# Row factors of the attention output through DRAM instead of through TensorE, and four buffers with another number of homes

## The reference

```python
q = (x @ Wq).reshape(B, T, H, 2 * DH)        # B 4, T 1024, H 16, DH 32
k = (x @ Wk).reshape(B, T, KV, 2 * DH)       # KV 4, each used by 4 query heads
v = (x @ Wv).reshape(B, T, KV, 2 * DH)
q1, q2, k1, k2 = halves of q and k, each rotated (RoPE)
a1 = softmax(q1 @ k1.T * scale + causal mask)
a2 = softmax(q2 @ k2.T * scale + causal mask)
out = (a1 - lam * a2) @ v
out = group norm over (T, 2 * DH) per head, * gn_w + gn_b
x = layernorm(x + (out * (1 - LAMBDA_INIT)) @ Wo)
up, gate = x @ ternary(W_up).T, x @ ternary(W_gate).T
x = layernorm(x + (silu(up) * gate) @ ternary(W_down).T)
```

## Time and profile before

| | |
|---|---|
| time, median of 3 runs | 2199.38 us (2192.79 to 2201.3) |
| the profiled execution, its own time | 2201.01 us |
| its span in the trace | 2196.6 us |
| TensorE busy | 2125.6 us, 97% |
| VectorE busy | 1688.4 us, 77% |
| ScalarE busy | 1458.0 us, 66% |
| GpSimd busy | 1194.4 us, 54% |
| mean granted clock of TensorE | 0.992 |

### The profile page before, as it was taken

How to read it: one execution, slowest core, us unless ns; L and a number is a source line. 1 busy time by engine, 2 the same in 40 slices (tenths; PEclk the granted TensorE clock), 3 DMA queues, 4 the chain that set the end, 5 groups by cost and what they waited for, 6 DMA issues and landing times.

```text
span 2196.6 us, 41181 instructions
## 1 busy us (share of the span) xinstructions
PE 2125.6 (97%) x13314; PEld 1367.8 (62%) x13314; DVE 1688.4 (77%) x3701; ACT 1458.0 (66%) x3450; POOL 1194.4 (54%) x1919
## 2 busy tenths in 40 slices
PE   8999999999999999999999999999999999999998
PEld 4666666666665766666666666666666666654443
DVE  4888888889888887788887888878778788853333
ACT  0777777667776777777667777777677687742232
POOL 0577666677655655555654655655455555531232
PEclk9999999999999999999999999999999999999999
DMA  7666576757655512212462322342552212114000
GB/s 252 200 210 219 195 216 198 238 180 221 189 163 149 163 51 61 92 50 62 145 153 79 97 68 84 96 125 73 154 116 54 73 40 87 49 49 110 6 20 19
DMA packets 291217, 263.85 MB, mean 120 GB/s; under 512 B 65088, under 2 KB 233152, under 8 KB 288960
## 3 DMA queue, kind: packets, MB, share of 16 engines
q1 hardware_dynamic: 279808, 228.65, 35.6%
q10 hardware_dynamic: 11200, 32.58, 4.6%
HBM read 181.48 MB, written 71.30 MB: 115 GB/s over the span
## 4 chain that ended last, share of the span: by engine, by line
PE 77%; DVE 8%; POOL 5%; issue 5%; ACT 4%; DMA 1%; ACTq 0%; DVEq 0%; SPq 0%; POOLq 0%
PE PS L1171 18%; PE PS L1120 11%; PE PS L1101 10%; PE PS L1082 10%; PE PS L1140 9%; PE PS L1161 9%; PE PS L1180 8%; PE PS L1147 2%; DVE e_long L1458 2%; POOL linv L1383 2%; ACT dt_long L1222 1%; ACT e_long L1232 1%; POOL coef L1384 1%; PE PS L1086 1%; DVE e_long L1524 1%
## 5 line engine op out<-in xcount | busy, mean ns | idle before, releaser
L1383 POOL TENSOR_TENSOR linv<-lsum,powers 128x2 f32<-128x2 f32 x512 | 405.7, 792 | 415.5 <-ACT e_long L1232 340.2
L1232 ACT ACTIVATE e_long<-e_long,nmax 128x768 f32<-128x768 f32 (+3 forms) x512 | 505.2, 987 | 159.5 <-DVE nmax L1458 156.8
L1458 DVE CUSTOM_DVE_ANT_0 e_long<-PS,mask_b 128x768 f32<-128x768 f32 (+3 forms) x512 | 516.8, 1019 | 82.1 <-PE PS L1101 61.0
L1101 PE MATMUL PS<-kstk,qstk 128*128 128x384 f32 (+5 forms) x1536 | 479.0, 416 | 19.6 <-DVE nmax L1458 9.5
L1101 PEld LDWEIGHTS PS<-kstk,qstk 128*128 128x128 f32 x1536 | 269.7, 191 | 144.5 <-issue 83.8
L1222 ACT ACTIVATE dt_long<-PS 128x512 f32<-128x512 f32 (+3 forms) x544 | 258.4, 514 | 136.5 <-PE PS L1082 126.5
L1524 DVE SCALAR_TENSOR_TENSOR e_long<-e_long,coef 128x1024 f32<-128x1024 f32 (+3 forms) x256 | 276.6, 1080 | 68.4 <-POOL coef L1384 68.0
L1232 ACT ACTIVATE e_short<-e_short,nmax 128x384 f32<-128x384 f32 (+3 forms) x512 | 283.1, 557 | 20.1 <-DVE nmax L1458 19.4
L1396 POOL TENSOR_TENSOR hid<-th,hid 128x512 f16<-128x512 f32 x128 | 148.2, 1160 | 248.8 <-ACT hid L1272 129.6
L1384 POOL TENSOR_SCALAR coef<-lsum,linv,neglam 128x1 f32<-128x1 f32 x512 | 233.2, 456 | 53.4
L1082 PE MATMUL PS<-ident,e_long 128*128 128x128 f32 x1664 | 239.6, 276 | 13.9 <-DVE nmax L1458 7.1
(11 more groups left out here) (117 smaller groups left out, 3114.9 us busy)
## 6 DMA issues: line engine op xcount, KB each, us to landing
qstk<-dq SPq DMA_DIRECT2D x512, 128.0 KB, 2.9
dq<-hl SPq DMA_DIRECT2D x25, 1024.0 KB, 5.1
wr<-in_w_proj ACTq DMA_DIRECT2D x48, 512.0 KB, 5.1
kstk<-dk SPq DMA_DIRECT2D x64, 256.0 KB, 5.2
da<-ra SPq DMA_DIRECT2D x32, 512.0 KB, 3.3
at_sb<-da SPq DMA_DIRECT2D x32, 512.0 KB, 4.3
wt<-in_w_up SPq DMA_DIRECT2D x16, 512.0 KB, 6.0
wt<-in_w_gate SPq DMA_DIRECT2D x16, 512.0 KB, 5.5
```

The source lines that it names most:

```text
L1101: last = nc.tensor.matmul(slot[:, h, :], qstk[:, duo % 4, 2 * r + m, :].bitcast(F32R), kstk[:, g % 2, m, h * w:(h + 1) * w].bitcast(F32R), ...
L1232: nc.scalar.activation(e, e, ACT.Exp, bias=nmax[:, u % 8:u % 8 + 1], scale=-1.0, accum_out=lsum[:, n % 4, m:m + 1]).then_inc(s_exp, 1)
L1383: link(nc.gpsimd.tensor_tensor(linv[:, a % 8, :], lsum[:, a % 4, :], mone, ALU.pow))
L1458: nc.vector.tensor_tensor_reduce(out, slot, mask, -1.0, -NEG, ALU.add, ALU.min, nmax[:, u % 8:u % 8 + 1]).then_inc(s_negmax, 1)
```

## The change

The columns of `linv` are no longer spread and transposed. SP stores the two columns of a duo to a row pair in DRAM (`store inverses`: 128 x 2 elements of 4 bytes), waits until they have landed, and loads each row of 128 factors into 64 partitions of `inverses` (`load inverses`: two DMAs, four homes). The product on VectorE reads them there, after a wait for the landing (`s_rows`). The POOL copy, the transposition, the extra block of the eviction and `r_short` are gone, and with them the waits of evictions for products. `e2_long` gets a second home, so that the minimum of a long head's second map waits for the combine two long heads back and no longer for that of the previous long head. `coef` gets four columns for two, `qstk` three homes for four, and `xT` four for six. The planner's durations and conditions follow, so that all five lists are made anew.

```diff
@@
-X_HOMES = 6
+X_HOMES = 4
@@
-    home = (4 * h + c + 4) % X_HOMES
-    return home, B - 1 if home < 4 else h
+    return c, B - 1 + h
@@
-            if STEPS[back].r:
-                out.append(ITEM("product", STEPS[back].duo))
-        if STEPS[a].r and not in_line(STEPS[a].duo) and STEPS[a].duo >= 8:
-            out.append(ITEM("product", STEPS[a].duo - 8))
@@
-            out.append(ITEM("combine", a - 2))
+            out.append(ITEM("combine", a - 2 if a % 2 or a < 4 else a - 4))
@@
-        out = [ITEM("values", run_of(a))]
+        out = [ITEM("values", run_of(a)), ITEM("load inverses", a)]
@@
+    elif what == "store inverses":
+        out = [ITEM("factor", heads_of(a)[1])] + [ITEM("load inverses", a - 4)] * (a >= 4)
+    elif what == "load inverses":
+        out = [ITEM("store inverses", a)] + [ITEM("product", a - 4)] * (a >= 4)
@@
-        if a >= 4:
-            out.append(ITEM("scores", heads_of(a - 4)[1], 1))
+        if a >= 3:
+            out.append(ITEM("scores", heads_of(a - 3)[1], 1))
@@
+            def store_inverses(duo):
+                second = heads_of(duo)[1]
+                sp.wait_ge(s_coef, second + 1)
+                sp.dma_start(dinv[duo].rearrange("r q -> q r"), linv[:, (second - 2) % 8:second % 8 + 1:2, 0],
+                             allow_slow_non_contiguous=True)\
+                    .then_inc(s_inv[duo % 4], 16)
+
+            def load_inverses(duo):
+                inverses_stored(sp, duo)
+                if duo >= 4:
+                    multiplied(sp, duo - 4)
+                for r in range(2):
+                    sp.dma_start(inverses[64 * r:64 * r + 64, duo % 4, :], dinv[duo, r:r + 1, :].broadcast_to((64, P)))\
+                        .then_inc(s_rows[duo % 4], 16)
@@
-                if blocks > keys:
-                    duo = STEPS[n].duo
-                    pe.wait_ge(s_wide, duo + 1)
-                    last = nc.tensor.transpose(F[bank][:, keys * P:blocks * P],
-                                               wide[:, duo % 2, :, :].rearrange("p r d -> p (r d)"), ident[:, :])
                 last.then_inc(s_tb, 1)
@@
-                if here < blocks:
-                    copied = nc.scalar.activation(r_short[:, :], F[bank][:, here * P:blocks * P], ACT.Copy)
@@
-                        nc.gpsimd.tensor_copy(wide[:, duo % 2, :, :], linv[:, (a - 2) % 8:a % 8 + 1:2, 0:1]
-                                              .broadcast_to((P, 2, 64))).then_inc(s_wide, 1)
@@
-                if m == 1 and n >= 2:
+                if m == 1 and n % 2 and n >= 2:
                     dve.wait_ge(s_comb, n - 1)
+                elif m == 1 and n >= 4:
+                    dve.wait_ge(s_comb, n - 3)
@@
-                    rows = dt_of(heads_of(a)[1])[:, t + 1, :] if in_line(a) else r_short[:, :]
+                    dve.wait_ge(s_rows[a % 4], 32 * (a // 4 + 1))
                     dve.wait_ge(s_pv, run_of(a) + 1)
```

More of the change, by code:

```diff
@@ L392, in after @@
         out = [ITEM("exponent", a, 1), ITEM("minus lambda")]
-        if STEPS[a].r and STEPS[a].duo >= 2:
-            second = heads_of(STEPS[a].duo - 2)[1]
-            out.append(ITEM("turn", second, turns(second) - 1))
+        if a >= 8:
+            out.append(ITEM("store inverses", STEPS[a - 8].duo))
+    elif what == "store inverses":
+        out = [ITEM("factor", heads_of(a)[1])] + [ITEM("load inverses", a - 4)] * (a >= 4)
+    elif what == "load inverses":
+        out = [ITEM("store inverses", a)] + [ITEM("product", a - 4)] * (a >= 4)
     elif what == "hidden low":
@@ L478 @@
            [ITEM("store rotated", j) for j in O_JOBS], [ITEM("load q", duo) for duo in range(DUOS)],
+           [ITEM("store inverses", duo) for duo in range(DUOS)], [ITEM("load inverses", duo) for duo in range(DUOS)],
            [ITEM("turn x", j) for j in OF_KIND["wo"]], [ITEM("load k", g) for g in range(B * KV)], [ITEM("load v", g) for g in range(B * KV)],
@@ L489 @@
 AHEAD = {"minimum": 1.0, "exponent": 1.0, "evict": 1.5, "factor": 2.0, "combine": 0.6, "empty": 3.0, "copy": 2.0,
-         "sum": -1.5, "ternary": -1.5, "side": -1.0, "rsqrt": 1.0, "product": 0.5, "load q": 2.0, "store rotated": 3.0}
+         "sum": -1.5, "ternary": -1.5, "side": -1.0, "rsqrt": 1.0, "product": 0.5, "load q": 2.0, "store inverses": 1.5, "load inverses": 1.5, "store rotated": 3.0}
 NTH = 4
@@ L745, in layer_kernel @@
         linv = sb("linv", [P, 8, 2])
-        coef = sb("coef", [P, 2])
-        dt_long = [sb(f"dt_long{r}", [P, NT + r, P]) for r in range(2)]
+        coef = sb("coef", [P, 4])
+        dt_long = [sb(f"dt_long{r}", [P, NT, P]) for r in range(2)]
         dt_short = sb("dt_short", [P, 3, NT // 2, P])
-        r_short = sb("r_short", [P, P])
-        wide = sb("wide", [P, 2, 2, 64])
+        inverses = sb("inverses", [P, 4, P])
         ra = sb("ra", [P, 2, T])
@@ L847, in layer_kernel @@
         s_pv = sem("s_pv")
-        s_wide = sem("s_wide")
+        s_inv = [sem(f"s_inv{k}") for k in range(4)]
+        s_rows = [sem(f"s_rows{k}") for k in range(4)]
         s_short = sem("s_short")
@@ L1046, in _ @@
                     load_q(a)
+                elif what == "store inverses":
+                    store_inverses(a)
+                elif what == "load inverses":
+                    load_inverses(a)
                 elif what == "load k":
@@ L1100, in scores @@
                 for h in range(parts):
-                    last = nc.tensor.matmul(slot[:, h, :], qstk[:, duo % 4, 2 * r + m, :].bitcast(F32R),
+                    last = nc.tensor.matmul(slot[:, h, :], qstk[:, duo % 3, 2 * r + m, :].bitcast(F32R),
                                             kstk[:, g % 2, m, h * w:(h + 1) * w].bitcast(F32R), start=True, stop=True)
```

70 lines of the change are left out of this document (28 added, 42 removed).

## The result

The changed kernel takes 3162.9 us (median of 4 runs, 3145.8 to 3187.0) against 2197.5 us; the ratio is 1.440, 95% interval 1.429 to 1.452. I had forecast 2172 us.

What follows compares the result with a forecast made beforehand. TensorE, busy 2125.6 of 2196.6 us, was taken as the bound. Less 28.2 us, all other terms 0, the span is 2168.4; plus 4.4 outside, less 1.6 for the median, 2171, rounded to 2172 us; range 2148 to 2203.

Steps and rivals of the forecast that it cites:

- the price of the store: Store of factors to DRAM: 2.1 us from issue to landing, within a trip of 5.6 us.
- Rival D: Store's 256 small elements go one after another at 45 ns, trip 17 us, VectorE stands: over 2500 us; chance 0.05.
- the DMA engines' share: DMA engines: 98 304 new packets at 45 ns, 277 us on each of 16 engines; room enough.
- TensorE's part: TensorE's list: 256 transpositions go at 0.11 us each, nothing takes their place: -28.2 us.
- The trip: Factors through DRAM to VectorE's product: 5.6 us, hidden under an even duo's 8.8 us lag; term 0.
- rival C: Late products hold up VectorE's minima, 192 us idle at 0.14 us each: +27 us, 2199 us; chance 0.17.
- Homes, 0: Changed homes for q, x and long second maps: loads still arrive in time, TensorE waits for none; 0.
- Rival B: Second home and freed evictions take away half of 44 us TensorE idle time: 2150 us; chance 0.14.
- Rival E: Three q homes and SP's in-order waits make TensorE wait for q, 51 us: 2223 us; chance 0.07.
- The tail, F: Feed-forward work moves into the tail, 97 to 100% busy, and costs nothing; no chance of its own.

Runs made afterwards that it cites:

- e5: The change with its stores issued but loads not waiting for them and reading another input; only the factor 8 heads later waits: 2739.7 us (1.247).
- e11: Kernel before with all lists unchanged, 192 of 256 transpositions of the spread factors left out: 2184.2 us (0.9942).
- e2: Kernel before with all homes of the change and lists made for them, factors still going through TensorE: 2254.0 us (1.0256).
- e1: The change without the store to DRAM and the wait for it; loads stay but read another input: 2229.9 us (1.0145).
- e16: Kernel before, four x homes, other lists kept, 192 transpositions out, SP given waited stores 64 bytes apart and loads of another input: 2252.4 us (1.0248).
- e9: Kernel before with four homes for x instead of six and nothing else changed: 2196.9 us (0.9997).
- e15: Kernel before with four x homes, two for long second maps and four coef columns, planner not told, lists kept: 2195.6 us (0.9988).
- e8: Kernel before with three homes for q instead of four and nothing else changed, lists made for it: 2213.6 us (1.007).
- e21: As e16, but with the change's own store of neighbouring elements and loads of the true factors: 3122.1 us (1.422).
- e12: e2 with the planner's PACE 3.85 instead of 3.75 us a head: 2251.3 us (1.0242).
- e6: The change with the store's 4-byte elements 64 bytes apart in DRAM, waiting loads reading another input: 2258.9 us (1.028).
- e13: The change's trip without its new homes, store elements 64 bytes apart, waiting loads reading another input, new lists: 2240.4 us (1.0197).
- e10: Kernel before with four x homes, two for long second maps and four coef columns, planner told, new lists: 2247.4 us (1.0234).
- e14: Kernel before with the planner's PACE 3.85 instead of 3.75 us a head: 2221.1 us (1.011).
- e23: Kernel before with the planner's PACE 3.76 instead of 3.75, only lists differing: 2203.8 us (1.0041).

## Why the prediction was wrong

**The step that failed is the price of the store.** I took 2.1 us from `out<-x`, with 3.3 us as the upper end, "because the store has only 1 KB". The change's store lands 9.9 us behind its issue in the median, and the whole trip of an even duo takes 17.5 us for my 5.6. Rows of large stores can't bound one of neighbouring 4-byte elements from above; bytes were the wrong measure to find the nearest row by. With elements 64 bytes apart the landing takes 2.4 us: for such a store 2.1 would have been near. Rival D, at 0.05, had the outcome (over 2500 us, from a landing more than 3 us late) and the wrong mechanism: it priced packets one after another at 45 ns, and they took 9 ns in parallel. The rule that I weighed, the Trainium skill's in "DMA: Bandwidth & Descriptors", section "Specifications", that transfers under 512 bytes make the DMA engine read, modify and write, did point the right way. But here transfers of 4 bytes are quick as soon as they lie 64 bytes apart, so the size alone doesn't make them slow. On this the measurement decides.

**What I had not counted: others behind the store.** I priced the DMA engines' share (45 ns a packet, 277 us each) and found room. Room there was (37.5% of the span against 35.6%), yet DMAs behind the stores land late, in the other queue too (e5). In time it is 397 us more on each engine (37.5% of 3144.0 us less 35.6% of 2196.6 us), though a small packet takes 9 ns and not 45: the other packets take longer.

**TensorE's part, -28.2 us:** right in sign, too large. e11 measured 13 us for 21, which makes some 17 for 28; e2 to e1 gives 24 with other lists. Reading 97% busy as the only bound left out that a shorter list waits more (7 us more idle time in e11).

**The trip, 0:** even with a quick store it costs 68 us over e11 with kept lists. "5.6 us is under 8.8 us" set a sum of medians against one duo's lag and left out the spread of both, and SP's standing for landings, 1428 us in the change and 263 us in e16, was priced at nothing. This was rival C's mechanism, mis-priced: C counted 0.14 us for each us that VectorE waits, and e16 loses 68 us with 56 us of such waits.

**Homes, 0:** right for x (e9) and for the second home as such (e15, -2 us), wrong for q (+15 us) and above all for the planner's answer to the second home (+52 us). I had compared the lists at one place and called them alike. Rival B, a gain from the second home, has no support. **Rival E**, TensorE waiting for q, is real: 30.0 us in e8 and, counted in the same way, 329.3 us in the changed kernel. There it takes the store and the third home together: 7.0 us in e1 without the store, 6.2 us in e21 with the store and four homes.

**The tail, F:** moved as said, at no cost of its own (e12).

One path through the runs is 2197 + 57 (homes, e2) - 24 (e1) + 29 (quick store, e6) + 904 (its elements side by side) = 3163 us. It closes because each step is the difference of two runs, and the small steps depend on the path: e13 was expected at 2202 from the same sums and came out at 2240. The large one doesn't: e16 to e21, with kept lists, gives 870 us.

**Still open:** what in the lists of e10 and e14 costs 52 and 22 us. e23 puts an unprovoked change of lists at 9 us; more isn't shown. e13 asks for no such cost: with new lists it is 12 us under e16, the same trip with the old ones (and with 64 transpositions more). What two neighbouring elements do to each other in DRAM is open too. No kernel here that computes everything beats the one before beyond e15's 2 us, and e11's 13 us are to be had only if the factors could come without the transposition.

## To carry to other kernels

Before a column of an SBUF tile is stored as a contiguous row of DRAM, one 4-byte element for each partition, measure the time until its semaphore comes, and what it does to all DMAs behind it, on the other queue too. In a queue worked in order, a wait for a landing is paid by everything behind it, so a DMA round trip belongs on a queue where nothing urgent follows (my advice; no run here moved it to another queue). And where a planner makes the lists, try an edit first with the old lists kept: that separated 2 us from 52.

## What the runs showed of the hardware that I had not expected

- 256 elements of 4 bytes, written as two rows of neighbours to DRAM, report their landing 9.9 us after the issue in the median, though in the stretch shown the packets are through in under 1 us; 64 bytes apart it is 2.4 us. Nothing between 4 and 64 bytes was tried.
- With such stores other DMAs land late on both queues: weights on ScalarE's queue, 5.1 us before, at 9.7 us in the changed kernel, 8.9 us in e5 and 6.8 us in e21, but at 4.7 us in e6.
- With the waits the granted clock of TensorE fell to 0.866 in the mean (e21: 0.870; e5: 0.912), while it was 0.98 or more in the profiled execution of every kernel here without the neighbouring store.
